# Reordering the opening transfers of a vision tower kernel, and moving two masked copies to a later stage

## What is computed

```python
ei, eo = sign(eps_in) * sqrt(abs(eps_in)), sign(eps_out) * sqrt(abs(eps_out))   # for each of two layers
W  = W_w + W_sw * (eo[:, None] * ei[None, :])        # 128 x 256
b  = W_b + W_sb * eo
g, inner = patches @ W1.T + b1, patches @ W2.T + b2
h  = (g * tanh(softplus(g)) * inner) @ W3.T + W3_b + position
h  = concat(cls, h)
h  = h + attention(layernorm(h), rel_k, rel_v)       # rel_v enters as einsum('bhqk,qkd->bhqd')
h  = h + experts(layernorm(h))
```

## Time and profile before

| | us |
|---|---|
| median of three runs | 262.07 |
| the three runs | 262.07, 262.08, 261.42 |
| the profiled execution, own time | 261.36 |
| its span, first to last instruction | 259.5 |
| PE busy in the span | 236.2 (91%) |
| DVE busy | 153.7 (59%) |
| ScalarE busy | 132.5 (51%) |
| GpSimd busy | 64.4 (25%) |

### The profile page before, as it was taken

How to read it: one execution, slowest core, us unless ns; L and a number is a source line. 1 busy time by engine, 2 the same in 40 slices (tenths; PEclk the granted TensorE clock), 3 DMA queues, 4 the chain that set the end, 5 groups by cost and what they waited for, 6 DMA issues and landing times.

```text
span 259.5 us, 6469 instructions
## 1 busy us (share of the span) xinstructions
PE 236.2 (91%) x2507; PEld 202.2 (78%) x2507; DVE 153.7 (59%) x485; ACT 132.5 (51%) x442; POOL 64.4 (25%) x104
## 2 busy tenths in 40 slices
PE   0989999899886788899999999999999999999994
PEld 0755656599754566677878999799999999999993
DVE  0496798844479999996367749625060605152463
ACT  1543137872179899994047894451708080807100
POOL 8930112087015556667132300000000000000000
PEclk9999999999999999999999999999999999999999
DMA  6970000000003407054000000000000000000015
GB/s 210 287 177 3 0 1 0 0 4 3 3 0 68 98 15 150 4 172 158 5 3 3 0 3 0 4 0 3 1 0 3 0 0 3 0 3 0 1 30 137
DMA packets 10938, 10.05 MB, mean 39 GB/s; under 512 B 1121, under 2 KB 9679, under 8 KB 10780
## 3 DMA queue, kind: packets, MB, share of 16 engines
q1 hardware_dynamic: 8412, 7.88, 11.2%
q10 hardware_dynamic: 1952, 1.41, 1.9%
q0 software_dynamic: 544, 0.35, 0.5%
HBM read 7.52 MB, written 2.11 MB: 37 GB/s over the span
## 4 chain that ended last, share of the span: by engine, by line
PE 63%; DVE 17%; issue 6%; ACT 4%; POOL 4%; DMA 4%; ACTq 1%; DVEq 0%; POOLq 0%
PE banks L1075 58%; DMA region_d<-in_L_tok_W_sw 4%; DVE top L824 4%; DVE stb L808 3%; POOL w_lo L405 2%; ACT region_e L541 2%; PE banks L1276 2%; POOL rstd L338 2%; DVE stb L728 2%; DVE region_c L849 2%; DVE stats L710 1%; DVE h L701 1%; PE banks L1396 1%; ACT w_hi L549 1%; PE banks L1085 1%
## 5 line engine op out<-in xcount | busy, mean ns | idle before, releaser
L1065 DVE SCALAR_TENSOR_TENSOR KT<-banks,vbd,KT 128x128 f32<-128x128 f32 (+1 forms) x136 | 38.0, 342 | 54.3 <-PE banks L1075 53.8
L563 ACT ACTIVATE region_d<-banks,vecs 128x416 f32<-128x416 f32 x80 | 45.5, 610 | 44.5 <-PE banks L1075 44.4
L1075 PE MATMUL banks<-w_all,region_d 128*128 128x128 f32 (+1 forms) x544 | 63.0, 275 | 0.0
L1075 PEld LDWEIGHTS banks<-w_all,region_d 128*128 128x128 f32 (+1 forms) x544 | 61.4, 187 | 1.2 <-ACT region_d L563 0.2
L541 ACT ACTIVATE region_e<-banks,ntop 128x64 f32<-128x64 f32 x128 | 38.7, 362 | 6.5 <-DVE ntop L832 3.5
L541 ACT ACTIVATION_READ_ACCUMULATOR region_e<-banks,ntop 128x1 f32 x128 | 31.8, 255 | 0.0
L1075 PE MATMUL banks<-x_hi,w_hi 128*128 128x416 f32 x80 | 29.9, 373 | 0.0
L1075 PE MATMUL banks<-x_lo,w_hi 128*128 128x416 f32 x80 | 28.2, 353 | 0.0
L1075 PE MATMUL banks<-x_hi,w_lo 128*128 128x416 f32 x80 | 28.2, 352 | 0.0
L1276 PE MATMUL banks<-kc,stb 128*128 128x128 f32 x64 | 10.5, 286 | 8.1 <-DVE stb L808 8.0
L1075 PEld LDWEIGHTS banks<-x_hi,w_hi 128*128 128x128 f32 x80 | 15.1, 188 | 2.4 <-issue 1.2
(11 more groups left out here) (217 smaller groups left out, 367.8 us busy)
## 6 DMA issues: line engine op xcount, KB each, us to landing
region_a<-in_x SPq DMA_DIRECT2D x2, 512.0 KB, 6.3
region_a<-in_x SPq DMA_DIRECT2D x1, 1024.0 KB, 10.7
out<-h SPq DMA_DIRECT2D x2, 512.0 KB, 5.6
h<-out SPq DMA_DIRECT2D x4, 256.0 KB, 4.5
w_sb<-in_L_ffn_W SPq DMA_DIRECT2D x1, 1024.0 KB, 5.6
region_d<-in_L_attn_rel_v SPq DMA_DIRECT2D x2, 260.0 KB, 10.0
out<-KT SPq DMA_DIRECT2D x6, 64.0 KB, 1.8
out<-KT ACTq DMA_DIRECT2D x6, 64.0 KB, 2.0
```

The costliest lines, as they stand in the source:

```text
L563: a.activation(HB[:, e % 2, s, blk * FB:(blk + 1) * FB], bank[h_bank(i)][:, 0:FB], ACT.Gelu, bias=vecs[:, v:v + 1]).then_inc(S["gelu_ok"], 1)
L1065: last = v.scalar_tensor_tensor(acc[0:m, t, :], bank[out_bank(u)][0:m, i * C:(i + 1) * C], comb[0:m, t, e:e + 1], acc[0:m, t, :], op0=ALU. ...
L1075: return t_.matmul(o, l, r, start=start, stop=stop)
```

## The change

- SP's queue takes all large transfers, in the order: first part of the pixels, the identity alone (128 columns of `kc`), `eps_in1`, second part of the pixels, W1 and its spread, second half of the pixels, `eps_in2`, W2 and its spread, the rest of the constants, Wq to Wo, `rvd`. No wait stands between them.
- ScalarE's queue keeps only small ones: both `eps_out`, now read straight into a column each (`eoc`), and four rows of biases. `eo` is made from `eoc` and no longer needs the turned rows.
- DVE's order in the front changes: the first product of root and sign and `evac_xT(1)` now stand ahead of `permute(0, 1)`; the second half's permutes stand ahead of the second weight.
- PE issues 2 in place of 5 `keep_warm` products between patches(0, 1) and patches(2, 3), turns the rows after the first weight, and has a new order of `embed1`: (0, 0), (0, 1), (1, 0), (1, 1), (0, 2) ahead of the class products, with (0, 3) after `embed3(0)`.
- ScalarE makes `root_sign(1)` after the copy of the first weight, ahead of the table load for Mish, and mish(0) and (1) ahead of `evac_xT(4)`.
- `RV` is made in the relative-key stage, one operation after each of the DVE copies of steps 1 and 2. `rvd` moves from `region_d` to a free part of `region_c`.

```diff
@@ SP
-            for r, b in ((V_EO1, eps_out1), (V_EO2, eps_out2), (V_B1, W1_b), (V_SB1, W1_sb), (V_B2, W2_b),
-                         (V_SB2, W2_sb)):
-                sp_.dma_start(rows[r:r + 1, :], b.unsqueeze(0)).then_inc(S["d_rows"], 16)
+                if half == 0:
+                    sp_.dma_start(ident, consts[:, K_ID:K_ID + P]).then_inc(S["d_const"], 16)
+                    sp_.dma_start(ei[:, 0:PIX], eps_in1.unsqueeze(0).to_broadcast([P, PIX])).then_inc(S["d_w1"], 16)
+            for i, w in enumerate((W1_w, W1_sw)):
+                sp_.dma_start(wprep[:, i, :], w).then_inc(S["d_w0"], 16)
+            sp_.dma_start(xraw[:, 1, :], xv[1]).then_inc(S["d_x2"], 16)
+            sp_.dma_start(ei[:, PIX:2 * PIX], eps_in2.unsqueeze(0).to_broadcast([P, PIX])).then_inc(S["d_w1b"], 16)
             for i, w in enumerate((W2_w, W2_sw)):
                 sp_.dma_start(wprep[:, 2 + i, :], w).then_inc(S["d_w2"], 16)
-            sp_.dma_start(xraw[:, 1, :], xv[1]).then_inc(S["d_x2"], 16)
+            sp_.dma_start(kc[:, P:K_ALL], consts[:, P:K_ALL]).then_inc(S["d_const2"], 16)
...
@@ ScalarE
-            a.dma_start(kc[:, :], consts).then_inc(S["d_const"], 16)
-            for i, v in enumerate((eps_in1, eps_in2)):
-                a.dma_start(ei[:, i * PIX:(i + 1) * PIX], v.unsqueeze(0).to_broadcast([P, PIX]))\
-                    .then_inc(S["d_w1"], 16)
+            for i, v in enumerate((eps_out1, eps_out2)):
+                a.dma_start(eoc[:, i:i + 1], v.unsqueeze(1)).then_inc(S["d_eo"], 16)
+            for r, b in ((V_B1, W1_b), (V_SB1, W1_sb), (V_B2, W2_b), (V_SB2, W2_sb)):
+                a.dma_start(rows[r:r + 1, :], b.unsqueeze(0)).then_inc(S["d_rows"], 16)
+            a.preload_act_table_set("sqrt_and_others")
...
-            act.wait_ge(S["d_w1"], 32)
+            act.wait_ge(S["d_eo"], 32)
+            link(a.activation(eo[:, 0:2], eoc[:, :], ACT.Abs))
+            a.activation(eo[:, 2:4], eo[:, 0:2], ACT.Sqrt).then_inc(S["eo_act"], 1)
+            a.activation(eo[:, 4:6], eoc[:, :], ACT.Sign).then_inc(S["eo_act"], 1)
+            act.wait_ge(S["d_w1"], 16)
             root_sign(0)
...
             a.activation(wnT[:, 0:256], bank[3][:, 0:256], ACT.Copy).then_inc(S["wnT_okA"], 1)
+            act.wait_ge(S["d_w1b"], 16)
+            root_sign(1)
             a.preload_act_table_set("mish")
+            mish(0)
+            mish(1)
             evac_xT(4)
-            mish(0)
             evac_xT(6)
...
@@ DVE, front
             permute(0, 0)
+            dve.wait_ge(S["eo_act"], 2)
+            v.tensor_tensor(eo[:, 6:8], eo[:, 2:4], eo[:, 4:6], ALU.mult)
+            dve.wait_ge(S["ei_act"], 2)
+            dve.wait_ge(S["d_w1"], 16)
+            link(v.tensor_tensor(ei[:, 0:PIX], ei_root[:, 0:PIX], ei_sign[:, 0:PIX], ALU.mult))
+            evac_xT(1)
             permute(0, 1)
...
+            perturb(0)
+            evac_xT(3)
+            dve.wait_ge(S["vec_ps"], 1)
...
             permute(1, 0)
             permute(1, 1)
-
+            dve.wait_ge(S["ei_act"], 4)
+            dve.wait_ge(S["d_w1b"], 16)
+            link(v.tensor_tensor(ei[:, PIX:2 * PIX], ei_root[:, PIX:2 * PIX], ei_sign[:, PIX:2 * PIX], ALU.mult))
+            perturb(1)
...
-            dve.wait_ge(S["d_rvd"], 32)
-            for s in range(2):
-                v.tensor_scalar(RV[:, :, s, :], rvd, kc[:, K_KP + s:K_KP + s + 1], None, ALU.mult)
@@ DVE, relative-key stage, after the copy of step i
+                if i in (1, 2):
+                    dve.wait_ge(S["d_rvd"], 32)
+                    v.tensor_scalar(RV[:, :, i - 1, :], rvd, kc[:, K_KP + i - 1:K_KP + i], None, ALU.mult)
@@ PE
             for t in range(2):
                 patches(t)
-            pe.wait_ge(S["d_rows"], 16 * 6)
-            pe.wait_ge(S["d_bias"], 16 * 4)
-            t_.transpose(bank[2][:, 0:NVEC], rows[0:NVEC, :], ident[0:NVEC, 0:NVEC]).then_inc(S["vec_ps"], 1)
-            keep_warm(5)
+            keep_warm(2)
             for t in range(2, 4):
                 patches(t)
...
             turn_weights(0)
+            pe.wait_ge(S["d_rows"], 16 * 4)
+            pe.wait_ge(S["d_bias"], 16 * 4)
+            t_.transpose(bank[2][:, 0:NVEC], rows[0:NVEC, :], ident[0:NVEC, 0:NVEC]).then_inc(S["vec_ps"], 1)
             keep_warm(2)
             pe.wait_ge(S["wnT_okA"], 1)
             embed1(0, 0)
+            embed1(0, 1)
             patches(4)
+            turn_weights(1)
             patches(5)
-            turn_weights(1)
-            embed1(0, 1)
+            pe.wait_ge(S["wnT_ok"], 1)
+            embed1(1, 0)
             patches(6)
             patches(7)
+            embed1(1, 1)
...
             embed1(0, 2)
-            pe.wait_ge(S["wnT_ok"], 1)
-            embed1(1, 0)
-            embed1(0, 3)
...
             embed3(0)
-            embed1(1, 1)
+            embed1(0, 3)
             embed1(1, 2)
```

43 lines of the change are left out of this document (13 added, 30 removed).

## The result

The kernel after takes 266.31 us (median of four, 264.98 to 266.4), the kernel before 262.07 (four, 261.42 to 262.19). The ratio is 1.0156, with a 95% interval of 1.0124 to 1.0187: 1.6% slower, where I forecast 0.3% faster with a range up to 261.9. The profiled execution of after has a time of 266.4 and a span of 264.6 us, against 261.36 and 259.5: 5.1 us to explain. Ratios in this document leave disturbed executions out (six of ten in the run with the memset late), so a median can stand higher than its ratio says.

A forecast was written before the change was run, and what follows sets the result against it. It took the front, fixed PE work started by W1's spread, to bound the kernel. Memset, permutes and second weight put X at 18.65 against 19.41, so 262.07 - 0.76 = 261.3 us; range 258.9 to 261.9.

The forecast's parts named there:

- The transfers' order and first landings: Front: identity lands at 5.4 us, W1's spread at about 8.7, and `embed1(0, 0)` can start at 12.0, before 14.67.
- Nothing earlier counts in this case: Front: with permutes waiting for POOL's memset, even a front 2 us slower ahead of it would still be covered.
- Rival 3: Transfers from one queue are slow: W2's spread landing after 16.5 us matters, after 17.3 eats gain; 262.0 to 263; chance 0.05.
- X: Point in the front when `embed1(1, 0)` can start: forecast 18.65 us against 19.41 before, gain 0.76.
- The permutes and the memset: Front: `permute(1, 0)`, ready at about 12.7 us, waits for POOL's memset until 14.85; both permutes then take 1.29.
- rival 1: Front: the second half's permutes do not wait for POOL's memset; X 16.8, gain 2.6 us, total 259.5; chance 0.32.
- my sign: Front: `permute(1, 0)` starting within 0.1 us of the memset's end, PE idle ahead of the second turned weight, would show the forecast.
- In the kernel before an idle microsecond at 12.7 did not lower the pace: Front: argument against a late rise of PE's clock, that one idle microsecond had left PE's pace as it was.
- My own sum: Front: memset ends 14.85, permutes 16.14, perturb(1) 17.53, weight turned 18.0, copied 18.6; X 18.65, gain 0.76 us.
- Rival 2: Front: PE's clock rises late, full rate only after X; X 22.3, 2.9 us slower, 265.0; chance 0.06.
- Every microsecond won or lost up to `embed(0)` to reach the end unchanged: Whole kernel: after `embed(0)` no transfer is late, so the 0.76 us gained in the front arrives whole at the end.
- `RV` for nothing: Relative-key stage: two operations of 1.29 us stay hidden, with 1.2 us to spare; cost 0, bounds 0 and 2 us.

The follow-up runs named there:

- the repetition: The kernel after, unaltered, measured once more: 265.89 us, ratio 1.0182.
- The three taken away together: The kernel after with fillers in the front, fillers in the attention loop and the second expert weight held: 264.95 us, ratio 1.0091.

## Why the prediction was wrong

1. **The transfers' order and first landings: right.** Identity 4.98 (forecast 5.4), patches(0, 1) over by 7.7, where the next products start (8.4), patches(2) 9.52 (9.95), `embed1(0, 0)` 11.58 (12.0), second half of the pixels 13.36 (12.6 to 13, a little late). The second part of the pixels and W1's spread landed at 8.7 and 9.5 (7.5 and 8.7), which cost little: patches(2) waited for DVE's order, and perturb(0) began at 9.49 for 10.0.
2. **"Nothing earlier counts in this case": wrong, and the first step that failed.** It rested on landings counted by bytes at 289 GB/s. `eps_in2` was in the 3.2 MB but had no landing of its own, and W2's spread was put near 14. Measured in after: `eps_in2` 15.9, W2's spread about 17.1. The product of root and sign started at 17.13 where I had 16.14: 0.71 us of that is the wait for the root, the rest the permutes, which ended at 16.42, since the memset began 0.43 later than before. W2's spread stood close behind: `perturb(1)` started at 17.59, and without the broadcast's wait it could have started no sooner than 17.1. The broadcast in SP's queue is part of that lateness, by a mean of about 1.4 us over the profiles, and not all of it; what the rest is stays open. Rival 3 asked for W2's spread after 16.5, at a chance of 0.05, and it came: its 262.0 to 263 is what the 0.26 us lost at X would have made, had nothing followed.
3. **The permutes and the memset: right.** They took 3.06 us for two beside the memset and 1.29 without it. So rival 1 falls. In all nine profiles of the new front with the memset in its place `permute(1, 0)` ended 0.54 to 0.55 us after it, though it began at anything from 12.81 to 13.80. The profile counts the wait into the copy (2.47 us from 13.36), so my sign, a start at the memset's end, could not show as I had worded it. The rule that I cited from the Trainium skill, SBUF — State Buffer, "SBUF: two separate sides", an exclusive lock for a whole instruction, agrees here: in after the memset ended at 15.28, the first permute at 15.82. The permutes came last only in the repetition, not in after: moving the spread made X 0.9 us earlier, moving the memset alone made no difference beyond the spread of profiles.
4. **X: 19.67 for 18.65.** A gain of 0.76 became a loss of 0.26; in the repetition X was 19.00, a gain of 0.41. Six profiles of this front lie between 19.00 and 19.89.
5. **"In the kernel before an idle microsecond at 12.7 did not lower the pace": true, and no ground for two.** My own sum had PE idle from 16.0 to 17.6 and priced it at nothing. PE waited 0.70 and 2.06 us, and the clock fell to 1.2 GHz for some 3.4 us: 1.25 us. Rival 2 came near on the right side (265.0) for the wrong cause, a rise that comes late, where it was a fall after waits: luck. The late rise itself did occur, in four profiles with the new front (`embed1(0, 0)` at 13.09 to 13.74 for 11.58), and cost no time at X, since the second weight came later still; it shortened PE's wait for that weight to 0.72 us or less, and in none of the four did the clock fall in the front. The Trainium skill, TensorE: Matmul & The Clock Gate, Part 1, has the array's clock at 1.2 GHz after idling and at 2.4 in sustained work; the rows agree.
6. **"Every microsecond won or lost up to `embed(0)` to reach the end unchanged": wrong, and the step that cost most.** The shift did stay rigid from 28 to 87 us, and arrived whole in the kernel before with 8 fillers. But 3.45 us came on top behind it: the loop (1.54, of which 0.21 is a longer wait and the rest the clock), where the clock falls in executions of before too, but in fewer of them (20 of 97 read a mean clock of 0.990 to 0.993, at 262.5 to 263.7 us; all but one of the rest read 0.996 or more), and PE's standing still (1.91 with it), which comes and goes from one execution to the next. The three taken away together did not bring the kernel back to my 262.2, so the account in after is of one execution and not a sum that was shown by undoing it.
7. **`RV` for nothing: right**, by itself 0.9999 (0.9978 to 1.0021).

What is shown: that the broadcast came last in after (its trace, and X earlier with it moved), the memset's part (moved, the permutes were short), and the front's clock (filled, the pace held, and 18 profiles agree). Supported, by one execution each, is that PE's standing still follows the transfers in place (moved with them, and made in the kernel before). That the instructions' own loading is what is late fits all seven stops, but the trace doesn't show PE's sequencer waiting for it. Open stays why W2's spread lands after 14 even with the broadcast elsewhere, what part GpSimd's transfers have in the low rate, why the clock falls in the loop in one execution and not in another with the same waits, what lengthens the second of them by 0.2 us, and why after meets the standing still in more of its profiles than before does.

## What to carry to other kernels

Give every transfer that someone waits for a landing of its own, and don't take it from bytes at one rate: one row of 1 KB spread over 128 partitions landed 2.6 us behind the 1 MB ahead of it and 1.4 behind the plain 128 KB that followed it, and the last of 3.2 MB came 3 us after its turn by bytes. Take several profiles of a kernel before reading half a microsecond from one: X of the same front moved by 0.9 us. When a sum leaves PE a wait of 1 to 2 us, price the clock after it as well as the wait, and fill the wait with products that take no longer than it. And read the profile beyond the point where the change ends: 3.4 of the 5.1 us arose some 60 us or more after the front.

## What the runs showed of the hardware

- While a broadcast of a 1 KB row to 128 partitions stood in SP's queue, all DMA engines together moved 87 to 169 GB/s for about 2 us, where they ran at 280 to 350 around it. With both broadcasts on ScalarE's queue, in the kernel before, the rate was 107 GB/s from 7 to 8 us; with only the second one there it landed in 6.5 us. What the broadcast does to the rate by itself isn't shown: GpSimd's transfers shared the low stretch of 12 to 13 us.
- Transfers of one queue can land out of order: W2 at 14.5 us, the broadcast issued ahead of it at 15.9.
- A 128x1024 fp32 copy of DVE within SBUF, ready during a GpSimd memset, ended 0.54 to 0.55 us after it in nine profiles of nine; alone it takes 0.69.
- TensorE's granted clock fell to 0.50 in the front after waits of 2.06 (0.70 shortly before it), 2.36, 2.10 and 1.98 us, and in none of the fourteen profiles with 1.75 or less; in the attention loop it fell after 0.71 and 1.61 to 1.65 us in eight profiles of ten.
- PE can stand still for 1.1 to 2.4 us with nothing that the profile shows to wait for. In the seven profiles with such a stop it went on 2.2 to 2.5 us after a 16 KB piece of instructions had started to move, beside 1 MB transfers of weights.
